# A normalising graph layer: where scales are made, who copies a kept product, and which bank holds a last block

## The reference

```python
h = jnp.maximum(_layernorm(x, axis=-1), 0.0)              # x: (64, 128, 1024)
# in the layer, xp = h as (N = 1024 nodes, B batches, T = 128)
x_avg = xs.mean(axis=1)
x_norm = x_avg / jnp.maximum(jnp.linalg.norm(x_avg, axis=-1, keepdims=True), 1e-12)
sim = (x_norm @ x_norm.T + 1.0) * 0.5
adj = (sim_flat + gumbel[:, 0] > 1.0 - sim_flat + gumbel[:, 1])
adj_sym = jnp.clip(adj + adj.T, 0.0, 1.0)
nmask = jnp.clip(adj_sym + jnp.eye(n), 0.0, 1.0)
common = nmask @ nmask.T
max_common = common.max()
valid = adj_sym * (common > 1.0) > 0
struct = jnp.where(valid, common / max_common * common, 0.0)
W = adj * struct
deg = W.sum(axis=0)
dinv = jnp.where(deg > 0, deg ** (-0.5), 0.0)
Wn = dinv[:, None] * W * dinv[None, :]
xw = jnp.einsum('nbt,to->nbo', xp, weight)                # weight: adj normalised by its absolute column sums
out = jnp.einsum('sd,sbt->dbt', Wn, xw) + bias
x = x + out
```

## Time and profile before

| | |
|---|---|
| median of 3 runs | 811.26 us |
| profiled execution | 810.59 us, span 808.8 us |
| busy in the span | TensorE 790.5, VectorE 549.7, ScalarE 501.0, GpSimd 307.0 us |
| granted TensorE clock | 0.999 of full speed |
| first pass (to 98 us) | DMA 404 to 423 GB/s |
| pairs 2 to 31 (from 191 us) | TensorE products and kept back to back |
| HBM | 78.18 MB read, 33.55 MB written |

### The profile page before, as it was taken

The page is one execution under the profiler, slowest core; times in us unless marked ns, Lnnn a source line. Parts: engine busy times, 40 slices in busy tenths (PEclk is TensorE's granted clock), DMA queues, the critical chain, the costliest instruction groups (busy, mean ns, idle before and its releaser), DMA issues.

```text
span 808.8 us, 14261 instructions
## 1 busy us (share of the span) xinstructions
PE 790.5 (98%) x5054; PEld 449.6 (56%) x5054; DVE 549.7 (68%) x668; ACT 501.0 (62%) x529; POOL 307.0 (38%) x391
## 2 busy tenths in 40 slices
PE   7989999999999999999999999999999999999997
PEld 7878766644555555554555455545554555455553
DVE  7999877999766656665666566656665666566652
ACT  4999966786665566555655566656555656566541
POOL 5667484301233333333333333333333333333320
PEclk9999999999999999999999999999999999999999
DMA  8999941007632323233322232223222322232112
GB/s 351 407 409 409 419 168 52 1 1 279 242 105 105 105 105 104 104 104 104 104 104 99 98 111 96 94 97 113 96 97 92 117 92 93 97 112 76 53 53 79
DMA packets 29983, 112.16 MB, mean 139 GB/s; under 512 B 3456, under 2 KB 3584, under 8 KB 28928
## 3 DMA queue, kind: packets, MB, share of 16 engines
q1 hardware_dynamic: 29952, 111.75, 37.5%
HBM read 78.18 MB, written 33.55 MB: 138 GB/s over the span
## 4 chain that ended last, share of the span: by engine, by line
PE 84%; DVE 3%; ACT 1%; issue 1%; POOL 1%; DVEq 0%; ACTq 0%; POOLq 0%
PE ps L1026 70%; PE ps L941 8%; PE ps L1042 2%; PE ps L959 2%; DVE xring L1209 1%; ACT zbuf L504 1%; DVE xring L1307 1%; DVE a L1314 1%; PE ps L810 0%; PE ps L832 0%; PE ps L894 0%; DVE a L1253 0%; POOL q_raw L477 0%; ACT hring L504 0%; DVE zbuf L1177 0%
## 5 line engine op out<-in xcount | busy, mean ns | idle before, releaser
L1026 PE MATMUL ps<-a,ybuf 128*128 128x512 f16 x2604 | 570.7, 379 | 1.2 <-DVE obuf L1402 1.0
L1026 PEld LDWEIGHTS ps<-a,ybuf 128*128 128x128 f16 x2604 | 252.6, 98 | 297.0 <-DVE obuf L1402 1.5
L1246 DVE TENSOR_TENSOR ybuf<-zbuf,ybuf 128x1024 f16<-128x1024 f32 x122 | 161.8, 1327 | 153.0 <-ACT ybuf L592 153.0
L466 POOL TENSOR_TENSOR zbuf<-zbuf 128x512 f32<-128x512 f32 x31 | 39.6, 1278 | 385.8 <-ACT zbuf L573 385.8
L592 ACT ACTIVATE ybuf<-zbuf 128x1024 f16<-128x1024 f32 x124 | 117.5, 949 | 110.4 <-POOL zbuf L473 97.9
L611 ACT ACTIVATE obuf<-ps,bias_sb,w_out 128x512 f32<-128x512 f32 x61 | 47.1, 772 | 112.7 <-PE ps L1026 112.7
L1235 DVE TENSOR_TENSOR hring<-hring 128x1024 f16<-128x1024 f32 x51 | 63.3, 1240 | 54.7 <-ACT hring L549 54.7
L471 POOL TENSOR_TENSOR zbuf<-zbuf 128x512 f32<-128x512 f32 x31 | 67.2, 2167 | 37.2 <-DVE a L1321 37.2
L941 PEld LDWEIGHTS ps<-w,hring 128*128 128x128 f16 x1224 | 72.6, 98 | 11.8
L1412 DVE TENSOR_TENSOR obuf<-obuf,xring 128x1024 f32<-128x1024 f32 x63 | 77.1, 1224 | 2.7
L941 PE MATMUL ps<-w,hring 128*128 128x128 f16 x1224 | 76.7, 219 | 0.0
(11 more groups left out here) (166 smaller groups left out, 685.8 us busy)
## 6 DMA issues: line engine op xcount, KB each, us to landing
xring<-in_x_dram SPq DMA_DIRECT2D x96, 512.0 KB, 4.8
out_dram<-obuf SPq DMA_DIRECT2D x63, 512.0 KB, 2.9
ybuf<-in_x_dram SPq DMA_DIRECT2D x28, 512.0 KB, 11.6
a<-in_L_gnn_gumbel_dram SPq DMA_DIRECT2D x7, 1024.0 KB, 19.5
obuf<-in_x_dram SPq DMA_DIRECT2D x9, 512.0 KB, 6.7
obuf<-in_L_gnn_gumbel_dram SPq DMA_DIRECT2D x1, 1024.0 KB, 26.5
out_dram<-obuf SPq DMA_DIRECT2D x2, 256.0 KB, 2.2
w<-in_adj_dram SPq DMA_DIRECT2D x1, 64.0 KB, 1.9
```

Of the source, the lines that this page charges most:

```text
L1026: mm = nc.tensor.matmul(bank[q % 2], y16[:, q % 2, yk, u, c * P:(c + 1) * P], a16[:, ak, mat, c, :], start=(start and c == yk == ak == 0), ...
L1246: nc.vector.tensor_tensor(y16[:, q % 2, 1, a:a + n, :], z[:, a + 1:a + 1 + n, :], y16[:, q % 2, 0, a:a + n, :], ALU.subtract).then_inc(s_y, 1)
```

## The change

The edits, part by part:

- ScalarE's table load is brought ahead of the loop by a copy of one column of zeros (`awake`).
- The copy of each trip's second kept product moves from ScalarE to VectorE (`keep_second`), at the end of VectorE's trip; three of them, in trips 0, 1 and 2.
- Degrees are scaled by `DEGREE_SCALE`; the scales come from the smallest degree rather than the largest root. The extreme value is transposed, reduced and spread ahead of the first root row; VectorE reads it twice into `least`, and GpSimd raises it to two powers and makes `kappa2` and `w_out`.
- `k0` is squared by GpSimd.
- `bound` becomes one instruction of another kind.
- All four of GpSimd's sums for pair 2 stand behind low part 14.
- The last block of pair 1 goes to `ps_a[0]` as a product of its own; ScalarE reads the rest of the block from `ps_b[1]` (behind `s_c` 14, between two copies of y), VectorE adds the two.
- TensorE waits in pair 2 for `s_c` 16 before it writes `ps_a[0]` again.

```diff
+            pool.wait_ge(s_k0, 1)
+            nc.gpsimd.tensor_tensor(k0[:, 1:2], k0[:, 1:2], k0[:, 1:2], ALU.mult).then_inc(s_k0, 1)
...
             roots(0, 0, HC)
             roots(1, HC, C)
-            z_sums(2, True)
+            pool.wait_ge(s_kap, 1)
+            nc.gpsimd.tensor_tensor(least_pow[:], least[:], halves2[:], ALU.pow).then_inc(s_kap, 1)
+            pool.wait_ge(s_k0, 2)
+            pool.wait_ge(s_kap, 2)
+            nc.gpsimd.tensor_tensor(kappa2[:], least_pow[:, 0:1], k0[:, 1:2], ALU.mult).then_inc(s_kap, 1)
+            pool.wait_ge(s_cnt, 2)
+            nc.gpsimd.tensor_tensor(w_out[:], least_pow[:, 1:2], w_count[:, 0:1], ALU.mult).then_inc(s_wout, 1)
+            pool.wait_ge(s_alo, 14)
+            z_sums(2)
...
+            act.wait_ge(s_wchain, 1)
+            nc.scalar.activation(awake[:], zeros[:, 0:1], ACT.Copy).then_inc(s_awake, 1)
...
-                    if j in KEEP_AFTER and not (isinstance(i, int) and j == KEEP_AFTER[1]):
-                        keep(NK * i + KEEP_AFTER.index(j))
+                    if j == KEEP_AFTER[0]:
+                        keep(NK * i)
...
             y_high(0, 2, 0)
             y_high(0, 2, 1)
+            act.wait_ge(s_c, 14)
+            nc.scalar.activation(o[1][1][:, LO], ps_b[1], ACT.Identity, bias=bias_sb[:, 0:1],
+                                 scale=w_out[:, 0:1]).then_inc(s_lower, 1)
             y_high(0, 2, 2)
             y_high(0, 2, 3)
...
-            first_xw(5, 0, HC)
+            first_xw(5, 0, 3)
+            turn(1)
...
             q_row(0)
-            first_xw(5, HC, HC + 2)
-            turn(1)
-            first_xw(5, HC + 2).then_inc(s_xw2, 1)
             spread(1)
+            first_xw(5, 3).then_inc(s_xw2, 1)
             pe.wait_ge(s_q, 2)
             q_row(1)
...
                 product(1, 5, 5, ps_b, False)
-                pe.wait_ge(s_c, 14)
                 made(6)
-                product(1, 2, 6, ps_b, False)
+                product(1, 2, 6, (None, ps_a[0]), True)
...
+                if isinstance(r, int) and r == 2:
+                    pe.wait_ge(s_c, 16)
                 product(q, 1, 1, ps_a, True)
...
+            def keep_second(i):
+                dve.wait_ge(s_xw1, NK * i + 2)
+                nc.vector.tensor_copy(xw_res[:, bass.ds(NK * i + 1, 1), :].rearrange("p a n -> p (a n)"),
+                                      ps_xw1).then_inc(s_xw1used, 1)
+
             for q in range(1, BODY1 // 2):
                 stats_of(0, q)
+            keep_second(0)
             with dve.Fori(1, TRIPS1 - 1) as i:
                 for q in range(BODY1 // 2):
                     stats_of(i, q)
+                keep_second(i)
...
-                nc.vector.tensor_scalar(degree_min[:, a:b], degree[:, a:b], TINY, None, ALU.max).then_inc(s_degmin, 1)
+                nc.vector.scalar_tensor_tensor(out=degree_min[:, a:b], in0=degree[:, a:b], scalar=0.0, in1=degree[:, a:b],
+                                               op0=ALU.is_le, op1=ALU.max).then_inc(s_degmin, 1)
...
             bound(1, HC, C)
+            dve.wait_ge(s_degmin, 4)
+            nc.vector.tensor_reduce(col2[:, 1:2], degree_min[:], AX_X, ALU.min).then_inc(s_colmax, 1)
             root(0, 0, HC)
+            top_of(1)
             root(1, HC, C)
-            dve.wait_ge(s_q, 2)
-            nc.vector.tensor_reduce(col2[:, 1:2], qf[:], AX_X, ALU.max).then_inc(s_colmax, 1)
+            dve.wait_ge(s_topb, 2)
+            nc.vector.tensor_scalar(least[:], ps_top[1][:, P:P + 1].broadcast_to([P, 2]), 1.0, None,
+                                    ALU.mult).then_inc(s_kap, 1)
...
-            nc.vector.reciprocal(q_inv[:], q_top[:]).then_inc(s_kap, 1)
...
-            nc.vector.tensor_tensor(kappa2[:], kappa[:], kappa[:], ALU.mult).then_inc(s_kap, 1)
...
                 dve.wait_ge(s_mm, 14 + 7 * r + 7)
+                if isinstance(r, int) and r == 1:
+                    dve.wait_ge(s_lower, 1)
+                    nc.vector.scalar_tensor_tensor(out=ob[:, LO], in0=ps_a[0], scalar=w_out[:, 0:1], in1=ob[:, LO],
+                                                   op0=ALU.mult, op1=ALU.add).then_inc(s_c, 1)
+                    return
```

More of the change, by code:

```diff
@@ L47 @@
 A_SCALE = 2.0 ** 14
-Q_MIN = 1e-6
+DEGREE_SCALE = 2.0 ** -24
 def gnn_kernel(nc, x, adj, bias, gumbel, out):
@@ L115, in gnn_kernel @@
         w_count = sb("w_count", [P, 2])
-        q_top = sb("q_top", [P, 1])
-        q_inv = sb("q_inv", [P, 1])
-        kappa = sb("kappa", [P, 1])
         kappa2 = sb("kappa2", [P, 1])
+        least = sb("least", [P, 2])
+        halves2 = sb("halves2", [P, 2])
+        least_pow = sb("least_pow", [P, 2])
         w_out = sb("w_out", [P, 1])
+        awake = sb("awake", [P, 1])
         w_abs = obuf[:, 2, 0:P]
@@ L194, in gnn_kernel @@
         s_w16 = sem("w16_ready")
+        s_awake = sem("scalar_engine_awake")
         s_bn = sem("bn_stats_done")
@@ L258, in gnn_kernel @@
         s_c = sem("block_read")
+        s_lower = sem("lower_part_of_pair_1_read")
         s_out = sem("out_ready")
@@ L377, in _ @@
             nc.gpsimd.memset(neg_eighth, -0.125).then_inc(s_pchain, 1)
-            pool.wait_ge(s_pchain, 8)
+            nc.gpsimd.memset(halves2[:, 0:1], 0.5).then_inc(s_pchain, 1)
+            nc.gpsimd.memset(halves2[:, 1:2], -0.5).then_inc(s_pchain, 1)
+            pool.wait_ge(s_pchain, 10)
             nc.gpsimd.affine_select(out=ident[:], in_=ones[:], compare_op=ALU.is_equal, fill=0.0, base=0,
@@ L386, in norms @@
                 a, n = groups_of(i)[g]
-                done = 8 + CHAIN * i + chain_before(g, i)
+                done = 10 + CHAIN * i + chain_before(g, i)
                 if not pooled(i, g):
@@ L719, in _ @@
             square(rows_hi, 0, 0, 1)
-            act.wait_ge(s_kap, 4)
+            act.wait_ge(s_kap, 3)
             high_rows(0, 0, rows_hi, 0, 0, 1)
@@ L1259, in degree_of @@
                 m = slice(c * P, (c + 1) * P)
-                nc.vector.scalar_tensor_tensor(out=squares[:, m], in0=ps_diag[:, m], scalar=1.0, in1=ident[:],
+                nc.vector.scalar_tensor_tensor(out=squares[:, m], in0=ps_diag[:, m], scalar=DEGREE_SCALE, in1=ident[:],
                                                op0=ALU.mult, op1=ALU.mult,
@@ L1325, in _ @@
             dve.wait_ge(s_qrow, 1)
-            rooted(rows_hi, 0, 0, 0)
-            top_of(1)
-            rooted(rows_hi, 0, 0, 1)
-            dve.wait_ge(s_topb, 2)
-            nc.vector.tensor_scalar(q_top[:], ps_top[1][:, P:P + 1], Q_MIN, None, ALU.max).then_inc(s_kap, 1)
-            dve.wait_ge(s_kap, 1)
-            nc.vector.reciprocal(q_inv[:], q_top[:]).then_inc(s_kap, 1)
-            dve.wait_ge(s_kap, 2)
-            dve.wait_ge(s_k0, 1)
-            nc.vector.tensor_scalar(kappa[:], q_inv[:], k0[:, 1:2], A_SCALE ** 0.5, ALU.mult,
-                                    ALU.mult).then_inc(s_kap, 1)
-            dve.wait_ge(s_kap, 3)
-            nc.vector.tensor_tensor(kappa2[:], kappa[:], kappa[:], ALU.mult).then_inc(s_kap, 1)
-            rooted(rows_hi, 0, 0, 2)
-            rooted(rows_hi, 0, 0, 3)
+            for c in range(HC):
+                rooted(rows_hi, 0, 0, c)
+            dve.wait_ge(s_qrow, 2)
+            rooted(rows_hi, 0, 1, 0)
             low_part(0, 0, rows_hi, 0, 0)
             low_part(0, 0, rows_hi, 0, 1)
-            dve.wait_ge(s_qrow, 2)
-            rooted(rows_hi, 0, 1, 0)
+            rooted(rows_hi, 0, 1, 1)
             low_part(0, 0, rows_hi, 0, 2)
-            rooted(rows_hi, 0, 1, 1)
             low_part(0, 0, rows_hi, 0, 3)
-            dve.wait_ge(s_bias, 16)
-            dve.wait_ge(s_cnt, 2)
-            nc.vector.tensor_scalar(w_out[:], q_top[:], q_top[:, 0:1], w_count[:, 0:1], ALU.mult,
-                                    ALU.mult).then_inc(s_wout, 1)
             def rooted_two(rows, k, half, part):
@@ L1449, in dve_pair @@
                 add_x(i, q, 1)
+            dve.wait_ge(s_wout, 1)
+            dve.wait_ge(s_bias, 16)
             upper0(0, 1)
```

11 lines of the change are left out of this document (5 added, 6 removed).

## The result

The changed kernel takes 813.03 us (median of 12 runs, 812.69 to 813.51), the kernel before beside it 811.06 (12 runs): ratio 1.0026, 95% interval 1.0018 to 1.0033. Its profiled execution took 813.07 us with a span of 811.4. It is 2.0 us slower; 813.4 with a range of 811.2 to 815.3 was forecast.

The account below looks back on a forecast made before the run. TensorE's start after VectorE's first pass and the degree stage was taken to set the time. Copies +2.9, scales -0.5, bank and sums -0.3 gave +2.1 us: 813.4 on the median, range 811.2 to 815.3.

Parts of the forecast that it names:

- Copies: First pass: three second kept copies moved onto VectorE, the pacemaker, cost +2.9 us, bounds +2.2 and +3.9.
- put back 0.3 in all for its own semaphore waits: First pass: 0.3 us added to the cost of the three moved copies for VectorE's semaphore waits.
- Table load: First pass: moving it ahead of the loop frees 3.8 us of ScalarE, worth nothing on the path.
- Scales: Degree stage: TensorE's start at 158.44 comes 0.5 us earlier, bounds -1.3 and +0.4.
- Bank and sums: Pairs 1 and 2: the removed bank wait gains 1.04 us, late GpSimd sums leave -0.3 of it.
- I take 0.7, nearer the short end, since VectorE itself stands waiting in part of it: Pair 2: a product gets its bank 0.4 to 1.4 us late behind GpSimd's sums; 0.7 was chosen.
- the late bound of 196.7: Pair 2: GpSimd's four sums, started near 189.2, end at 195.7, or 196.7 if the third takes 2.28 us.
- The bound of +0.4: Upper bound on the bank and late sums term, forecast at -0.3 us; the lower bound was -1.04.
- "same": Rival, chance 0.18: loop heads hide more and GpSimd's sums finish in time; +0.7 us, 811.9.
- "faster": Rival, chance 0.10: ScalarE paces the first pass, VectorE's statistics having hidden waits; -2.8 us, 808.4.
- "The sums lock out": Rival, chance 0.10: every GpSimd sum between 189 and 197 us waits out a two-input VectorE step; +4.3, 815.6.
- "VectorE stands for the product": Rival, chance 0.06: VectorE waits 0.5 us or more each trip for TensorE's kept product; +3.6 or more, 815 to 817.

Follow-up runs that it names:

- e8: Kernel before with the table load ahead of the loop and the three second kept copies on VectorE; 812.53 us, ratio 1.0024.
- e3: Kernel before with only the table load moved ahead of the loop; 811.00 us, ratio 1.0002.
- e4: Changed kernel with GpSimd's first two sums for pair 2 put back ahead of the wait for low part 14; 811.71 us, ratio 1.0011 to before.
- e5: Changed kernel with the second kept copies back on ScalarE and GpSimd's first two pair 2 sums early again; 808.34 us, ratio 0.9971 to before.
- e2: Kernel before with only the three second kept copies moved to VectorE, table load still in the loop; 812.81 us, ratio 1.0028.
- e9: Kernel before with one unread 128x1 fill added to VectorE's program where it waits for the first load; 809.74 us, ratio 0.9988.
- e12: e5 with GpSimd's two early sums made to wait for the sixth low part; 808.03 us, ratio 0.9966 to before.
- e10: Kernel before with four unread 128x1 fills added to VectorE's program where it waits for the first load; 809.88 us, ratio 0.9988.

## Why the prediction was right, and where its parts were not

By the four stretches, changed less before: the profiled execution started 0.44 later; 94.20 - 91.62 = +2.58; -0.74; +0.27; -0.01. That is 2.54 in the span; without the later start it is 2.1, and the medians say 2.0. Forecast was +2.1. The sum came this near partly by luck: the copies cost 0.4 less than forecast and the scales gave 0.2 more, the bank and the sums came out 0.6 worse, and these errors cancelled.

- **Copies: +2.9 forecast, +2.5 found** (2.53 at the boundaries, 2.46 in e8). VectorE paces the pass, two loop heads of 0.40 are hidden, a copy costs 1.14 to 1.2: all as put. The step that failed is "put back 0.3 in all for its own semaphore waits": without the clock dip no copy waited.
- **Table load: 0 forecast, 0 found** (e3).
- **Scales: -0.5 forecast, -0.74 found.** The first rooted row is at 150.53, 3.44 later than in the earlier trace rows; with 3.02 for the later copy of batch 2 that is +0.42, as forecast (+0.4). ScalarE does set the stretch: VectorE waits for it at 157.16. With the sums early (e4, e5) the gain is 61.84 - 61.38 = 0.46. The other 0.28 comes from the sums being out of the way, which the working named (two low parts in 2.43 us) and then held to be hidden behind ScalarE.
- **Bank and sums: -0.3 forecast, +0.27 found.** The bank's own gain was nearly right (1.22, with 1.04 put). The step that failed is "I take 0.7, nearer the short end, since VectorE itself stands waiting in part of it": the late sums give back 1.49. They ended at 199.37, by the earlier clock (TensorE's 72 matmuls start 2.28 later) 197.1, 0.4 behind the late bound of 196.7. And only the path to a bank of pair 2 was looked at, not who needs the second sum: ScalarE's copy of y (195.53) and behind it VectorE's (the `ybuf` of the 0.87 wait), a product earlier. So the wait that was expected, of some tenths for the bank, came (0.3), and a larger one ahead of it that was not expected. The prediction also numbers these products wrongly: the four in the 10.53 us of the earlier trace rows begin with the last of pair 1, so its "third" and "fourth" of pair 2 are the second and the third. The bound of +0.4 did hold it.
- **Of the rivals**, "same" failed on the sums and "faster" on the statistics, which never waited. "The sums lock out" was right in kind: two sums of four took 2.1 to 2.2 us, not all, so it cost tenths and not 1.4 more. "VectorE stands for the product" came true in e2 alone, under a clock dip.

The line of 0.2% above which the prediction speaks of "slower" is passed by little: 0.26%, and the lower end of the interval, 0.18%, lies under it. What the change is worth by itself is not hurt by the 0.7 us of the last stretch, since it and the kernel before both carry it.

## What to carry to other kernels

Before a wait is removed, look for the next one that hangs on work moved in the same edit, and follow every product of that work to the first engine that needs it: here four sums behind a common wait swallowed the whole gain of a bank that was correctly freed. Moving a step from an engine that waits to the engine that paces costs its full length, less only the issue time that it hides. Below 0.1% of a long kernel, compare the stretches of the traces and not the medians alone, since an unrelated instruction can move the end.

## What the runs showed of the hardware that was not expected

- **A useless instruction of 0.06 us made the kernel 1 us faster** (e9: 809.74 against 810.82). 0.7 us of it stands between the start of the last block and the end of the span; that stretch takes only the values 32.8 and 32.1 in 14 kernels.
- **The loop head's issue idle (0.39 to 0.40 us) is gone behind a long instruction.** With a copy of 1.17 to 1.23 us ahead of the branch the next statistics start 1.09 to 1.14 us after the copy starts, as between any two neighbours.
- **Who is stretched when GpSimd and VectorE meet depends on the moment.** In the kernel before two low parts, each reading two operands from SBUF, took 2.43 us beside the sums, and 1.42 without; the first, begun at 150.62 ahead of the second sum (150.83), took its 0.74, the second, begun at 151.28, took 1.76. In e12 the low part at 161.21 takes its 1.28, and GpSimd's sum that begins 0.2 us behind it 2.21, where the same sum took 1.67 in the kernel before. The Trainium skill ("SBUF — State Buffer", section "Who interferes with whom") has both halves: such a pair excludes each other, and the order of issue decides who is blocked. The trace agrees.
- **A clock dip cost time in one kernel and none in another.** Both e2 and e10 have it in the profiled execution at 14 to 18 us, after TensorE had been busy 0.95 and 1.49 of 4 us. In e10, with the copies on ScalarE, the first stretch is 91.39 and nothing is lost; in e2 VectorE waits, and it is 95.53.
- **With ScalarE's table load ahead of the loop no dip came.** None of the nine profiled kernels with the early load had one, two of the five with the load in the loop had. Of the other executions only a mean clock is listed: over all of them it is 0.998 or less, as in those two, in 33 of 134 with the load in the loop and in none of 87 with it ahead. Two pairs differ by the load alone: e3 has it in none of 10, the kernel before beside it in 5 of 31; e8 in none of 11, e2 in 3 of 8. In the profiled executions TensorE is busy for 0.95 to 2.25 of the 4 us from 10 to 14 us with the load in the loop, and for 2.45 to 3.96 with it ahead. That the early load keeps the dip away is strongly suggested by this; no run was made to test it, and its gain is small (e3's median is that of before).

The row of e10 with its dip, columns as in the earlier trace rows:

```profile
14.00:18.00 4.00, 4.00 (x24) 4.00 (x23) 3.87 (x9) 2.15 (x2) 3.29 (x14) 0.60 1.03 410
```
